# Softmax weights of a windowed attention divided before the value product, by VectorE sums and GpSimd, in a fused SSM, MoE and attention kernel

## What is computed

```python
x = x + ssm(layernorm(x))         # projection, conv, scan over tokens, projection
x = x + moe(layernorm(x))         # 8 experts, 128 -> 512 -> 128, silu(g) * u, mixed by a router
x = x + attention(layernorm(x))   # 16 heads of 8 channels
x = x + moe(layernorm(x))         # the same weights again

# attention, the part that the change touches
scores = jnp.einsum('bhsd,bhtd->bhst', q, k) + chunk_attention_mask(S)   # chunks of 10, 25 keys to the left
probs = jax.nn.softmax(scores, axis=-1)
out = jnp.einsum('bhst,bhtd->bhsd', probs, v)
```

## Time and profile before

| | |
|---|---|
| time, median of 3 runs (lowest, highest) | 1492.82 us (1489.45, 1494.48) |
| the profiled execution's own time | 1493.85 us |
| its span, first to last instruction | 1492.1 us |
| mean granted PE clock over the span | 0.994 |
| busy: PE, PEld | 1427.2 us (96%), 1236.2 us (83%) |
| busy: DVE, ACT, POOL | 950.3 us (64%), 773.0 us (52%), 504.3 us (34%) |
| chain that ended last | PE 77%, DVE 10%, ACT 5%, issue 5%, POOL 4% |

### The profile page before, as it was taken

The page is one execution under the profiler, slowest core; times in us unless marked ns, Lnnn a source line. Parts: engine busy times, 40 slices in busy tenths (PEclk is TensorE's granted clock), DMA queues, the critical chain, the costliest instruction groups (busy, mean ns, idle before and its releaser), DMA issues.

```text
span 1492.1 us, 31350 instructions
## 1 busy us (share of the span) xinstructions
PE 1427.2 (96%) x12756; PEld 1236.2 (83%) x12756; DVE 950.3 (64%) x2125; ACT 773.0 (52%) x1037; POOL 504.3 (34%) x446
## 2 busy tenths in 40 slices
PE   5798999999999999999999999999999999999998
PEld 3587878888788888888888888888888888888887
DVE  5655686665856667567675785658755565566543
ACT  6364738653466545645456574555644444355321
POOL 4351553433423443135410671136503320331000
PEclk9999999999999999999999999999999999999999
DMA  5120341004210420124002500062004200510000
GB/s 170 52 58 15 102 123 31 16 15 121 40 38 23 135 40 1 45 99 83 9 2 81 137 8 9 2 164 61 1 2 121 40 2 1 138 24 2 1 7 8
DMA packets 82876, 75.50 MB, mean 51 GB/s; under 512 B 5532, under 2 KB 60860, under 8 KB 82732
## 3 DMA queue, kind: packets, MB, share of 16 engines
q1 hardware_dynamic: 82732, 73.50, 18.8%
HBM read 60.65 MB, written 12.83 MB: 49 GB/s over the span
## 4 chain that ended last, share of the span: by engine, by line
PE 77%; DVE 10%; ACT 5%; issue 5%; POOL 4%; DMA 1%; DVEq 0%; SPq 0%; POOLq 0%; ACTq 0%
PE pd L1003 25%; PE pg L275 7%; PE pu L275 7%; PE pg L277 6%; PE pu L276 6%; PE pg L276 6%; PE pu L277 6%; PE att_ps L680 3%; DVE h L1096 2%; PE att_ps L702 2%; POOL arena L631 1%; PE att_ps L707 1%; DVE ffn_rows L298 1%; POOL arena L633 1%; DVE x L1084 1%
## 5 line engine op out<-in xcount | busy, mean ns | idle before, releaser
L1058 ACT ACTIVATE h<-pg 128x512 f32<-128x512 f32 x512 | 303.5, 597 | 658.3 <-PE pg L277 655.2
L1003 PEld LDWEIGHTS pd<-w_down,h 128*128 128x128 f32 x4096 | 512.2, 192 | 31.8 <-issue 2.7
L1003 PE MATMUL pd<-w_down,h 128*128 128x128 f32 x4096 | 525.0, 276 | 0.8 <-DVE x L1084 0.8
L1096 DVE TENSOR_TENSOR h<-h,pu 128x512 f32<-128x512 f32 x512 | 345.5, 679 | 215.4 <-PE pu L277 213.9
L275 PE MATMUL pg<-ffn_x_hi,w_gate_hi 128*128 128x512 f32 x512 | 244.5, 477 | 1.5 <-DVE ffn_x_lo L358 1.5
L275 PE MATMUL pu<-ffn_x_hi,w_up_hi 128*128 128x512 f32 x512 | 205.3, 401 | 13.4 <-DVE h L1096 13.2
L276 PE MATMUL pu<-ffn_x_lo,w_up_hi 128*128 128x512 f32 x512 | 203.3, 397 | 0.0
L276 PE MATMUL pg<-ffn_x_lo,w_gate_hi 128*128 128x512 f32 x512 | 203.3, 397 | 0.0
L277 PE MATMUL pg<-ffn_x_hi,w_gate_lo 128*128 128x512 f32 x512 | 203.0, 397 | 0.0
L277 PE MATMUL pu<-ffn_x_hi,w_up_lo 128*128 128x512 f32 x512 | 202.9, 396 | 0.0
L905 POOL TENSOR_TENSOR att_arena<-att_arena 128x512 f32<-128x512 f32 (+1 forms) x72 | 72.8, 1011 | 352.6 <-DVE att_arena L777 352.3
(11 more groups left out here) (192 smaller groups left out, 1540.2 us busy)
## 6 DMA issues: line engine op xcount, KB each, us to landing
arena<-bc_spread SPq DMA_DIRECT2D x56, 256.0 KB, 4.8
att_arena<-v_rows SPq DMA_DIRECT2D x64, 144.0 KB, 4.0
qk_rows<-qk_parts SPq DMA_DIRECT2D x32, 256.0 KB, 2.3
q<-qk_rows SPq DMA_DIRECT2D x32, 256.0 KB, 3.6
k<-qk_rows SPq DMA_DIRECT2D x32, 256.0 KB, 4.5
att_arena<-v_rows SPq DMA_DIRECT2D x64, 128.0 KB, 3.4
arena<-in_x SPq DMA_DIRECT2D x8, 256.0 KB, 2.9
x<-in_x SPq DMA_DIRECT2D x8, 256.0 KB, 3.4
```

The costliest lines, as they stand in the source:

```text
L1003: last = nc.tensor.matmul(pd[:, t * P:(t + 1) * P], h_b[:, d % NH, t * P:(t + 1) * P], wd[:, d % NCH, :], start=d % CPE == 0 and t == 0, s ...
L1058: nc.scalar.activation(h_b[:, c % NH, :], pg[c % 2][:, :], ACT.Silu).then_inc(gate_done, 1)
L1096: nc.vector.tensor_tensor(h, h, pu[d % 2][:, :], ALU.mult).then_inc(h_done, 1)
```

## The change

The sums over the keys are no longer products with ones. VectorE sums the exponentials of a unit along its rows and takes the reciprocals of the 8 sums (`sums`, at n + 1, where `turned` was). GpSimd multiplies the weights by the reciprocals in place (`weights`, at n + 1 + 1/8). Only then VectorE turns them (`turned`, now at n + 1 + 1/2), PE multiplies them by the values (at n + 1 + 3/4 instead of 3/8), and VectorE copies the result out (`out`, a step later, at n + 2). The tile `ones`, its fills at the start and `divided` go. Two new semaphores, `s_sum` and `p_norm`, order the three engines.

```diff
--- before.py
+++ after.py
@@ -166,9 +166,7 @@
 
         attT = att_ar[:, o1:o1 + L]
         o1 += L
-
-        ones = sb("ones", [P, 4 * HD])
-        rsum = sb("r_sums", [P, 2 * QW])
+        rsum = sb("r_sums", [P, 2, 4])
         smax, = (att_ar[:, o1 + 8 * i:o1 + 8 * i + 8].rearrange("p (w g) -> p w g", w=2) for i in range(1))
         xn_att = att_ar[:, 0:L].rearrange("p (t d) -> p t d", t=TT)
 
@@ -211,6 +209,7 @@
         v_zero, v_pad, v_out, v_moved, p_t = sem("v_zero"), sem("v_pad"), sem("v_out"), [sem(f"v_moved{i}") for i in range(2)], sem("p_t")
         q_set, v_set = sem("q_set"), sem("v_set")
         s_max, s_sub, s_exp, x2_bias = sem("s_max"), sem("s_sub"), sem("s_exp"), sem("x2_bias")
+        s_sum, p_norm = sem("s_sum"), sem("p_norm")
         act_step, dve_step, pool_step = sem("act_step"), sem("dve_step"), sem("pool_step")
 
         class Chain:
@@ -689,7 +688,7 @@
                     if n + 1 < NUNIT:
                         yield at(n + 1 + 1 / 8)
                         scores(n + 1)
-                    yield at(n + 1 + 3 / 8)
+                    yield at(n + 1 + 3 / 4)
                     if n in (0, NW // 4):
                         pe.wait_ge(v_set, 4 * j + (4 if n else 2))
                     name = ("o", j, n)
@@ -699,14 +698,9 @@
                     for i, w in enumerate(UNITS[n]):
                         for v in range(2):
                             for g in range(4):
-                                nc.tensor.matmul(ps[32 * g:32 * g + 32, i * QW:(i + 1) * QW],
-                                                 v_w[:, w, v, 32 * g:32 * g + 32], pt[n % 2][:, i, g, v, :],
-                                                 start=(i, v) == (0, 0), stop=False)
-                        for v in range(2):
-                            for g in range(4):
-                                last = nc.tensor.matmul(ps[32 * g:32 * g + 32, (2 + i) * QW:(3 + i) * QW], ones[:, :],
-                                                        pt[n % 2][:, i, g, v, :], start=False,
-                                                        stop=(w, v) == (UNITS[n][-1], 1))
+                                last = nc.tensor.matmul(ps[32 * g:32 * g + 32, i * QW:(i + 1) * QW],
+                                                        v_w[:, w, v, 32 * g:32 * g + 32], pt[n % 2][:, i, g, v, :],
+                                                        start=(i, v) == (0, 0), stop=(w, v) == (UNITS[n][-1], 1))
                     ab.fill(last, name)
                 yield Att.end(j) + 2
                 ps = ab.take(pe, ("proj", j))
@@ -776,30 +770,39 @@
                         dve.wait_ge(s_sub, NUNIT * j + n)
                     nc.vector.reduce_max(smax[:, 0:nw, :], s_u[n % 2][:, 0:nw, :, :], AX).then_inc(s_max, 1)
 
+                def sums(n):
+
+                    nw = len(UNITS[n])
+                    dve.wait_ge(s_exp, NUNIT * j + n + 1)
+                    if j or n:
+                        dve.wait_ge(p_norm, NUNIT * j + n)
+                    link(nc.vector.reduce_sum(rsum[:, 0:nw, :], s_u[n % 2][:, 0:nw, :, :], AX))
+                    nc.vector.reciprocal(rsum[:, 0:nw, :], rsum[:, 0:nw, :]).then_inc(s_sum, 1)
+
                 def turned(n):
 
                     nw = len(UNITS[n])
                     u = s_u[n % 2][:, 0:nw, :, :]
-                    dve.wait_ge(s_exp, NUNIT * j + n + 1)
+                    dve.wait_ge(p_norm, NUNIT * j + n + 1)
                     if n >= 2:
                         ab.wait(dve, ("o", j, n - 2))
                     nc.vector.transpose(pt_flat[:, n % 2, 0:nw * 4 * WK],
                                         u.rearrange("p w g k -> p (w g k)")).then_inc(p_t, 1)
 
-                def divided(n):
+                def out(n):
                     nw, name = len(UNITS[n]), ("o", j, n)
                     nq = WQ if nw == 2 else QW
                     ab.wait(dve, name)
-                    link(nc.vector.reciprocal(rsum[:, 0:nw * QW], ab.ps(name)[:, 2 * QW:(2 + nw) * QW]))
-                    ps, rs = (a.rearrange("p (w q) -> p w q", q=QW)[:, :, 0:nq]
-                              for a in (ab.ps(name)[:, 0:nw * QW], rsum[:, 0:nw * QW]))
+                    ps = ab.ps(name)[:, 0:nw * QW].rearrange("p (w q) -> p w q", q=QW)[:, :, 0:nq]
                     to = attT[:, 2 * n * WQ:2 * n * WQ + nw * nq].rearrange("p (w q) -> p w q", q=nq)
-                    ab.free(nc.vector.tensor_tensor(to, ps, rs, ALU.mult), name)
+                    ab.free(nc.vector.tensor_copy(to, ps), name)
 
                 for n in range(NUNIT + 1):
                     if n:
                         yield at(n)
-                        turned(n - 1)
+                        sums(n - 1)
+                        if n > 1:
+                            out(n - 2)
                     if n < NUNIT:
                         yield at(n + 1 / 4)
                         if n >= 2:
@@ -808,8 +811,10 @@
                         yield at(n + 3 / 8)
                         maxima(n)
                     if n:
-                        yield at(n + 5 / 8)
-                        divided(n - 1)
+                        yield at(n + 1 / 2)
+                        turned(n - 1)
+                yield Att.end(j)
+                out(NUNIT - 1)
                 yield Att.end(j) + 2.5
                 ab.wait(dve, ("proj", j))
                 dve.wait_ge(x2_bias, j + 1)
@@ -893,9 +898,19 @@
                     nc.gpsimd.tensor_tensor(v, v, pk("head").unsqueeze(1).unsqueeze(3)
                                             .broadcast_to([P, (w1 - w0) * 8, 4, HD]), ALU.mult).then_inc(v_set, 1)
 
+                def weights(n):
+                    nw = len(UNITS[n])
+                    u = s_u[n % 2][:, 0:nw, :, :]
+                    pool.wait_ge(s_sum, NUNIT * j + n + 1)
+                    nc.gpsimd.tensor_tensor(u, u, rsum[:, 0:nw, :].unsqueeze(3).broadcast_to([P, nw, 4, WK]),
+                                            ALU.mult).then_inc(p_norm, 1)
+
                 queries(0)
                 for n in range(NUNIT):
                     nw = len(UNITS[n])
+                    if n:
+                        yield Att.at(j, n + 1 / 8)
+                        weights(n - 1)
                     if n + 1 < NUNIT:
                         yield Att.at(j, n + 1 / 4)
                         queries(n + 1)
@@ -907,6 +922,8 @@
                     for part in {0: (0, 1), 2: (2,), 3: (3,)}.get(n, ()):
                         yield Att.at(j, n + 3 / 4 + part % 2 / 8)
                         like_heads(part)
+                yield Att.at(j, NUNIT + 1 / 8)
+                weights(NUNIT - 1)
 
         def pad_v(sp, link, k):
 
@@ -976,7 +993,7 @@
                     if c == 0:
                         pe.wait_ge(w_lo, 2 * E)
                         pe.wait_ge(wd_loaded, 16 * E)
-                        pe.wait_ge(pads_set, 8)
+                        pe.wait_ge(pads_set, 3)
                     if c < NC:
                         m = c // NCH
                         if c % NCH == 0:
@@ -1153,11 +1170,6 @@
                 nc.gpsimd.memset(half[:, :], -0.5).then_inc(pads_set, 1)
                 nc.gpsimd.memset(attT[0:32, 0:P], 0.0).then_inc(v_zero, 1)
                 pool.wait_ge(v_zero, 1)
-                nc.gpsimd.memset(ones[:, :], 0.0).then_inc(pads_set, 1)
-                pool.wait_ge(pads_set, 2)
-                for r in range(4):
-                    nc.gpsimd.memset(ones[32 * r:32 * r + 32, HD * r:HD * (r + 1)], 1.0).then_inc(pads_set, 1)
-                pool.wait_ge(pads_set, 6)
                 for buf in (k3[:, :, 0:LEFT], k3[:, :, LEFT + L:NKEY]):
                     nc.gpsimd.memset(buf.bitcast(F32), 0.0).then_inc(pads_set, 1)
                 interleave([(Ssm.pool, i) for i in range(B)] + [(Att.pool, j) for j in range(B)]
```

## The result

The changed kernel takes 1482.53 us in the median of 6 runs (1479.0 to 1484.45); the kernel before, beside it on the same chip, took 1493.62 us in 6 (1489.45 to 1494.76). The ratio is 0.9928 [0.9915, 0.9942], 10.8 us less. A later set of runs on one chip gave 0.9931 [0.9912, 0.9951] with a median of 1482.71. So the kernel is faster by 0.7%, inside the range, 4.5 us above the forecast of 1478. The two profiled executions, 1493.85 and 1479.00, differ by 14.9: that pair alone would have confirmed the sum to a tenth of a microsecond, and misled.

A forecast was written before the change was run, and what follows sets the result against it. PE's queue was taken to bound the kernel, with about 30 us of waiting for VectorE. Terms -20.4 (PE), +0.5 (place), +2 (VectorE), +3 (GpSimd's product) gave -15, so 1478 us, range 1469 to 1488.

The forecast's parts named there:

- About 30 us are VectorE being late, and almost all the rest is PE working: Whole span: PE waits about 30 us for VectorE's `h` and the convolution; otherwise it works through its queue.
- 20.4 us off PE: Attention blocks on PE: 2176 passes go, 0.30 us per full and 0.15 per half unit, 20.4 us less.
- The "swallowed" rival: PE reaches the next up product earlier and waits for `h`; stalls grow 10 to 20 us, result 1484 to 1495; chance 0.14.
- Block's place +0.5: PE's attention block moves from 3/8 to 3/4 of a step later; waits before blocks cost 0.5 us more.
- VectorE +2: VectorE's new sums, reciprocals and copies add 21 us busy time, mostly hidden; 2 us booked where PE waits for `h`.
- The new product +3: GpSimd's 72 added products hold VectorE instructions; about half of that reaches PE, costing 3 us.
- +6 us: VectorE work held by GpSimd's added products, in proportion to busy time over instruction groups: 4.7 us, say 6.
- The clock, 0: PE's stretches at granted clock 0.50 cost 3.4 us each; one could be lost or gained, so 0 booked.
- four or more: Sign in the profile after: the prediction is wrong if PE's clock stretches at 0.50 become four or more.
- The signs: Profile after: PE busy 15 to 20 us less, VectorE near 970, GpSimd near 577, `h` and L511 waits 30 to 38.
- The slower rival: GpSimd's product holds VectorE at L584/L585 and L298, deciding from 14 further places at 1.06 us each; chance 0.06.
- The sum: All terms together: -20.4 + 0.5 + 2 + 3 = -15 us, giving 1478 us.

The follow-up runs named there:

- e1: The kernel before without the products with ones, its reciprocal reading the result's own columns: ratio 0.9912 to the kernel before, 13.1 us off.
- e2: The changed kernel with the products with ones put back, their result unused: ratio 1.0026 to the kernel before, 3.9 us slower.
- e3: The changed kernel without GpSimd's product, so the weights stay unnormalized: ratio 0.9907 to the kernel before, 13.9 us off.
- e4: The kernel before with 72 GpSimd products of the same shape added on a spare tile, which nothing waits for: ratio 1.0028, 4.2 us slower.
- e7: The changed kernel with the product of weights and reciprocals on VectorE in place of GpSimd: ratio 1.0004 to the kernel before, 0.6 us slower.

## Why the prediction was right, step by step

The direction, the size and most signs held, but two terms were off to opposite sides and hid each other in part. In the prediction's own order:

- **"About 30 us are VectorE being late, and almost all the rest is PE working".** The 30 are right, the rest is not: PE's weight loads stood idle for 102.9 us in all, 34 of them in the first 56 us and 16.1 before blocks. It did no harm here, since most of that did not move.
- **"20.4 us off PE".** The computation was exact: 20.5 measured. The step from there to the end, "a microsecond taken off PE's queue is a microsecond off the span", failed by a third: 13.1 to 14.6 arrive (e1, e2). It excepted the places where VectorE is "about to be the later one", and then booked nothing for them. PE already waited there; a pause with a block shortly ahead of it swallows that block's 0.3 us. The "swallowed" rival had this mechanism; its price, 10 to 20 us, was too high, about 5 to 7 being right. This is the term that was mis-sized.
- **Block's place +0.5, VectorE +2.** Together nothing that can be measured (e3 against e1, 0.8 us the other way). The waits before the blocks did grow more than the +0.5, from 16.1 to 20.7 us; e3 has 19.9 where e1 has 16.9. But the waits for `h` are shorter in e3 (21.9 us, 23.8 in e1), so that all pauses together differ by 1.2.
- **The new product +3.** Measured 3 to 5 (e3) and 4.2 (e4). The size was nearly right, the reason too narrow. Held VectorE work grew where it hurts (the scan's mean 1528 from 1466, the mixing chain) and fell where it doesn't (L298 546 from 622), so the sum over groups, "+6 us", isn't what was paid. The Trainium skill (SBUF — State Buffer, "Who interferes with whom") says that a VectorE instruction with two SBUF inputs can be held by a GpSimd instruction that reads SBUF, and one with a single input, outside the 2-port modes, can't. The trace agrees at 1306 us instruction by instruction: L370, L371 and L373 are held (1.04, 0.94, 0.87 us), L372 and L374 are not (0.17, 0.18). The second route, GpSimd's own lateness for the SSM step, the prediction did not have.
- **The clock, 0.** On the average of runs no change that I can show for the changed kernel, two stretches in one profile and four in the next. The sign "four or more" was met in the second without the theory being wrong: as a sign it was too weak, since single executions of one kernel differ by it. In e7, with more long pauses, it is a real term.
- **The signs.** PE's busy time fell by 21.0, just more than the 15 to 20 announced, at 95%; waits for `h` and the convolution 34.7 us (30 to 38); GpSimd 577.0; VectorE 962.5 against "near 970".
- **The slower rival** (14 more held places that reach PE) did not come about: 25 waits for `h` in place of 20.
- **The sum.** With the measured terms: -20.5, +6 to +7 swallowed, 0 for VectorE and place, +3 to +5 for the product: -8.5 to -11.5, with -10.8 measured. The forecast of -15 was 4.5 us too good by the median. That the profiled pair gave 14.9 was luck: in it 20.5 came off the blocks, 11.6 went into pauses, and 3.4 of clock and 2.5 of the rest came on top.
